# A post-LayerNorm layer whose SBUF buffers start at other offsets: products' operands at multiples of 2,048 bytes

## The reference

```python
q = (x @ Wq.T + bq).reshape(B, S, H, D)      # k, v alike; H = 16, D = 32; q, k get rotary
qk = jnp.einsum('bshd,bstd->bsht', q, k) / jnp.sqrt(jnp.float32(D))
att = jax.nn.softmax(qk, axis=-1)
out = jnp.einsum('bsht,bstd->bshd', att, v)
out = jnp.swapaxes(out, 1, 2).reshape(B, S, E)
x = _layernorm(x + out @ Wo.T + bo)
g = jnp.einsum('th,ih->ti', xf, gate_w) * gate_s
u = jnp.einsum('th,ih->ti', xf, up_w) * up_s
hdn = jax.nn.silu(g) * u
x = _layernorm(x + jnp.einsum('ti,hi->th', hdn, down_w) * down_s)
```

## Time and profile before

| | |
|---|---|
| three runs | 1808.6, 1810.26 and 2465.16 us, median 1810.26 |
| profiled execution | 1810.45 us, of it the span from first to last instruction 1808.7 us |
| TensorE clock over the span | 0.981 of full |
| busy: TensorE, VectorE, ScalarE, GpSimd | 96%, 76%, 52%, 45% of the span |
| DMA | 278 MB, 154 GB/s over the span |

### The profile page before, as it was taken

The page is one execution under the profiler, slowest core; times in us unless marked ns, Lnnn a source line. Parts: engine busy times, 40 slices in busy tenths (PEclk is TensorE's granted clock), DMA queues, the critical chain, the costliest instruction groups (busy, mean ns, idle before and its releaser), DMA issues.

```text
span 1808.7 us, 40710 instructions
## 1 busy us (share of the span) xinstructions
PE 1731.1 (96%) x15138; PEld 1412.3 (78%) x15138; DVE 1375.9 (76%) x1976; ACT 943.2 (52%) x1458; POOL 809.2 (45%) x697
## 2 busy tenths in 40 slices
PE   4799999999999999999789999999999999999997
PEld 3677888888888888888568888888888888788785
DVE  5587999999999999999745766667666676667656
ACT  4354555555556555655534555455555545555453
POOL 5587888888888888888100110201102011020111
PEclk8799999999999999999989999999999999999998
DMA  5747668767786778678564353553436435254241
GB/s 162 150 96 168 163 154 177 175 162 155 172 175 167 158 165 176 169 161 209 165 208 148 117 178 96 184 167 126 153 96 203 148 130 164 82 200 148 92 164 70
DMA packets 447479, 278.20 MB, mean 154 GB/s; under 512 B 261440, under 2 KB 385984, under 8 KB 447424
## 3 DMA queue, kind: packets, MB, share of 16 engines
q1 hardware_dynamic: 447424, 277.50, 57.3%
HBM read 184.10 MB, written 93.32 MB: 153 GB/s over the span
## 4 chain that ended last, share of the span: by engine, by line
PE 91%; issue 3%; SPq 1%; DVE 1%; ACT 1%; DMA 1%; POOL 1%; POOLq 0%; ACTq 0%; DVEq 0%
PE ps_x L582 13%; PE ps_x L586 12%; PE ps_x L583 12%; PE ps_s L715 8%; PE ps_s L720 8%; PE ps_x L715 7%; PE ps_x L720 7%; PE ps_x L726 4%; PE ps_x L730 4%; PE ps_s L659 3%; PE ps_a L616 3%; PE ps_s L726 2%; PE ps_a L730 2%; PE ps_a L726 2%; PE ps_s L730 2%
## 5 line engine op out<-in xcount | busy, mean ns | idle before, releaser
L582 PE MATMUL ps_x<-wqkv_hi,xc_hi 128*128 128x512 f32 x768 | 307.1, 400 | 19.6 <-POOL xc_lo L1061 8.0
L586 PE MATMUL ps_x<-wqkv_hi,xc_lo 128*128 128x512 f32 x768 | 302.6, 394 | 0.0
L583 PE MATMUL ps_x<-wqkv_lo,xc_hi 128*128 128x512 f32 x768 | 302.5, 394 | 0.0
L1171 POOL TENSOR_TENSOR z<-z,xr 128x512 f32<-128x512 f32 x60 | 77.4, 1319 | 496.6 <-DVE z L1436 496.6
L715 PE MATMUL ps_s<-x_hi,slot 128*128 128x512 f32 x672 | 268.1, 399 | 7.9 <-ACT hid L949 4.5
L720 PE MATMUL ps_s<-x_lo,slot 128*128 128x512 f32 x672 | 265.5, 395 | 0.0
L861 ACT ACTIVATE kX<-kT 32x512 f32<-32x512 f32 x256 | 160.7, 628 | 188.2 <-DVE kT L1242 185.9
L1082 POOL TENSOR_TENSOR qk_cos<-qk_in,rot 128x512 f32<-128x512 f32 x128 | 202.4, 1581 | 83.2 <-DVE qk_in L1221 65.4
L715 PE MATMUL ps_x<-x_hi,slot 128*128 128x512 f32 x560 | 222.5, 397 | 6.7 <-ACT u L978 3.7
L720 PE MATMUL ps_x<-x_lo,slot 128*128 128x512 f32 x560 | 220.8, 394 | 0.0
L1088 POOL TENSOR_TENSOR qk_cos<-qk_cos,qk_sin 128x512 f32<-128x512 f32 x128 | 205.4, 1605 | 10.0
(11 more groups left out here) (112 smaller groups left out, 3724.6 us busy)
## 6 DMA issues: line engine op xcount, KB each, us to landing
slot<-gu_hi SPq DMA_DIRECT2D x88, 896.0 KB, 5.1
xc<-x_cols SPq DMA_DIRECT2D x32, 512.0 KB, 5.4
v_rows<-v_in SPq DMA_DIRECT2D x32, 512.0 KB, 4.2
v<-v_rows SPq DMA_DIRECT2D x32, 512.0 KB, 5.2
res<-x_rows SPq DMA_DIRECT2D x64, 256.0 KB, 3.5
x_rows<-x_out SPq DMA_DIRECT2D x32, 512.0 KB, 2.8
x_cols<-x_turn SPq DMA_DIRECT2D x128, 128.0 KB, 2.6
wide<-x_cols SPq DMA_DIRECT2D x64, 256.0 KB, 5.1
```

The lines of the kernel that those rows point to most:

```text
L582: pe.matmul(out, hi[:, k], w_hi[w][:, k], start=(k == 0), stop=False)
L583: pe.matmul(out, hi[:, k], w_lo[w][:, k], start=False, stop=False)
L586: last = pe.matmul(out, lo[:, k], w_hi[w][:, k], start=False, stop=(k == KE - 1))
L1171: pool.tensor_tensor(z[:, h, r], z[:, h, r], xr[:, r], ALU.add).then_inc(z_added[h], 1)
```

## The change

Only the order in which buffers are declared changes. The instructions of every engine, their order and their waits are the same as before, row by row; what differs is the addresses in them.

```diff
         inexact = sb("inexact", [P, 1], mybir.dt.int32)
-        wide = sb("wide", [P, 2, 4, E])
-        slot0 = sb("slot0", [P, OPS, HALF], F32R)
         gu_scale = sb("gu_scale", [P, 2, NJ])
...
         own4 = sb("own4", [P, A4])
-        rot = sb("rot", [P, 2, 2, D])
         stats = sb("stats", [P, 2, 6])
...
         ones = sb("ones", [P, 1])
+        to_line = sb("to_line", [P, 112])
+        wide = sb("wide", [P, 2, 4, E])
         w_raw = raw = wide
...
             prob = sb("prob", [P, 2 * Q32, H], F32, early)
-            top, total, over = (sb(name, [P, 2 * Q32], F32, early) for name in ("top", "total", "over"))
             pT = sb("pT", [P, 2, C * B4, Q32], F32, early)
...
         h1 = sb("h1", [P, 2, E], F32R)
-        rest1 = sb("rest1", [P, 3, 2 * Q32])
         h2, h3 = sb("h2", [P, 2, E], F32R), sb("h3", [P, 2, E], F32R)
         xr = sb("xr", [P, ROWS, E])
+        slot0 = sb("slot0", [P, OPS, HALF], F32R)
+        rot = sb("rot", [P, 2, 2, D])
+        top, total, over = (sb(name, [P, 2 * Q32]) for name in ("top", "total", "over"))
```

## The result

The changed kernel takes 1800.73 us (median of 5 runs, 1798.35 to 1802.78) where the kernel before takes 1809.81: a ratio of 0.9953, 95% interval 0.994 to 0.9965, that is 9.1 us or 0.5% less. One of the five executions of the kernel before took 2465.16 us and is not in the ratio. The forecast was 1,802.5. Its size and its place were right. Its reason, a border within 64 bytes, was not, as the experiments show.

The account below looks back on a forecast made before the run. The prediction took the distance between TensorE matmuls to bound the kernel. From 1,810.45 us it subtracted 7.9 us for slot0 and nothing for other operands, engines or DMA, giving 1,802.5 us, range 1,797 to 1,811.

Parts of the forecast that it names:

- a border within 64 bytes: Large matmuls: operands starting off a multiple of 64 are slow; only slot0 did, costing 9 ns a matmul.
- What bounds the kernel: Whole kernel: the distance between TensorE matmuls sets the time, while VectorE keeps its spare 8% in attention.
- Part 1: Feed-forward stage: slot0's matmuls reach the other slots' distance once at a multiple of 2,048; 7.9 us gained, bounds 5.5 to 8.4.
- 3 x 0.26 + 0.2: Gain per super step, in us: 0.26 for each of chunks 3, 6 and 9, and 0.2 for chunk 0.
- Part 2: Other large matmul operands, both stages: moving to multiples of 512 or 2,048 gains nothing; bound 92 us.
- the number of matmuls in a window: Attention's 200 us window: over 2,554 matmuls there would show that the other operands' starts gained time after all.
- Part 3: VectorE, ScalarE and GpSimd operands: new addresses change nothing; VectorE's 1,220 and GpSimd's 1,581 ns stay.
- Part 4: DMA targets: offsets change within 256 bytes; loads landing tenths of a microsecond earlier are covered by TensorE's work, gain nothing.
- A: Large matmuls: the start of moving or all operands costs 13.3 ns each; expected 1,710 to 1,740 us, chance 13%.
- B: slot0 in the feed-forward stage: low place or chunk turn, not address, makes it slow; 1,810 us, chance 9%.
- The rule of 16-byte cachelines: SBUF starts: a multiple of 32 is as good as 2,048, so moving slot0 gives nothing; 1,810 us.
- C: Attention, GpSimd and VectorE: operands with one remainder clash and slow the kernel to 1,830 to 1,850 us; chance 3%.

Follow-up runs that it names:

- e1: Kernel before with only slot0 declared 32 bytes later, at 192 of 2,048: 1808.12 us, ratio 0.9995 to the kernel before.
- e3: Changed kernel with everything from wide on 32 bytes later, so all large matmul operands start 32 past a multiple of 64: 1801.2 us, 0.9957 of before.
- e2: Changed kernel with slot0 alone 32 bytes later, 32 past a multiple of 2,048: 1807.92 us, ratio 0.9992 to the kernel before.
- e5: Kernel before with only slot0 declared behind z_shift, at 576 of 2,048: 1801.2 us, ratio 0.9961 to the kernel before.
- e6: Changed kernel with slot0's seven weight tiles at a pitch of 1,056 instead of 1,024 bytes: 1803.91 us in one run.
- e8: Kernel before with the chunks of moving operand wd at a pitch of 2,080 instead of 2,048 bytes: 1813.19 us in one run, against 1808.06 before.

## Why the prediction was right, and where it was not

**What bounds the kernel.** Right. TensorE's distance between starts sets the time, and every effect that was found acts through it. VectorE (183.81 of 200 us in the same window of attention, 183.32 before) and the others have not moved.

**Part 1, slot0.** The size was right: a super step lost 1.00 us where the sum had 3 x 0.26 + 0.2 = 0.98. It is earned in seven super steps, not eight: from the first to the second it was 139.1 us before and is 139.3; attention's rest is mixed in there. In the thirteen traces that stretch takes 137.1 to 139.8 us, so a gain of 1 us in it would not be seen. So the term is 7.0 us as far as it is shown, where 7.9 were taken; the prediction's lower bound had allowed for this. The reason was wrong. The step that failed is "what sets `slot0` apart is its address", 32 past a multiple of 64. The rows could not tell that from another reading, since `slot0` was at the same time the only stationary operand whose distance from its moving one was no multiple of 256 (96, against 0 and 256). The prediction looked at addresses one by one and never subtracted them. e1, at a multiple of 64 and slow, and e3, off it and fast, show it. That the size came out all the same is luck in one respect: the change also brought `slot0` and `x_hi` to one remainder, for which the prediction had no reason. e1 fulfils its rule without that and was 0.7 us under the kernel before, within the noise.

**Part 2, all other operands.** Nothing was taken and nothing came: attention's twelve matmuls from 508.58 to 511.30 us in the changed kernel take the same 2.72 us.

```profile
508.58 0.39 PE L582 MATMUL ps_x<-wqkv_hi,xc_hi 128*128 128x512 f32 x1
508.81 0.39 PE L583 MATMUL ps_x<-wqkv_lo,xc_hi 128*128 128x512 f32 x1
...
511.30 0.39 PE L582 MATMUL ps_x<-wqkv_hi,xc_hi 128*128 128x512 f32 x1
```

The argument for it, that these operands respect a border of 64 already, falls with part 1; the right one is that all of them lay at one remainder of 256 before too, 64. The sign that the prediction named beside it, the number of matmuls in a window, was a poor one: the window of 300 to 500 us holds 2,675 matmuls instead of 2,554, only because 128 more of the small ones of line 616 fall into it; of the large ones it holds 754 instead of 760.

**Part 3, the other engines.** Right, nothing:

```profile
L1422 DVE TENSOR_TENSOR x_lo<-wide,x_hi 128x1024 fp32r<-128x1024 f32 x32 | 38.9, 1220 | 1.3 <-ACT x_hi L997 1.3
L1082 POOL TENSOR_TENSOR qk_cos<-qk_in,rot 128x512 f32<-128x512 f32 x128 | 202.5, 1582 | 81.9 <-DVE qk_in L1221 63.9 <-DVE kT L1242 18.0
```

**Part 4, DMA.** Not contradicted for the time, and blind to what happens. The loads of `slot0` and the other slots, of `xc` and of `v` land 0.3 to 0.8 us earlier in the median (below), under cover of TensorE's work.

**The other 2 us.** The profiled executions differ by 9.8 us, of which super steps give 7.0. The feed-forward stage began at 874.1 us before and at 871.2 after. In the other profiled kernels of this study it began anywhere from 869.0 to 874.0, and in three executions of the full change at 871.2, 873.2 and 869.0. e1, with the late landings of the old layout, began at 872.6, not later than the repeated full change beside it with 873.2. This part is scatter of a single execution as far as the runs show.

**The rivals.** A fell: the matmuls stayed at 226.7 ns, in e3 and at multiples of 2,048 alike; what the 13.3 ns over 213.3 are is still open. B, that the address is not the cause, fell in its form of place and turn (e2 has the new place and is slow, e5 the old region and is fast), yet it came nearest to the truth in that the address by itself isn't the cause. The rule of 16-byte cachelines from the Trainium skill, "SBUF — State Buffer", section "Door 1: The DMA port swizzle", was set beside it: a start at a multiple of 32 is indeed as good as one at 2,048, as e3 shows, but two such starts 32, 96 or 128 bytes apart cost 7 to 9 ns a matmul, of which that rule tells nothing. C did not occur.

## What to carry to other kernels

Keep the stationary and the moving operand of a stream of matmuls at one remainder of 256 bytes; at the remainders 0, 32 and 64 that were run it made no difference where both lie, and 2,048 is not needed. One small tensor declared ahead of a weight buffer can cost 3 to 4% of each matmul that reads the buffer, with no wait that tells it, rows that read 0.40 instead of 0.39 us, and a busy time of 199.9 of 200 us either way; the distance between starts, compared between buffers, shows it. When an outlier has a special address, subtract it from the addresses that it is used with before believing in the address itself, and test by moving all together, then one alone.

## What the runs showed of the hardware beside that

That a distance costs anything was not foreseen: 7 to 9 ns of 226.7 in fp32r matmuls of 128 by 512 columns, gone at 256 bytes. Why, no run shows; reads of the two operands that get into each other's way would do that, but this is only argued. One thing in the traces bears on it: with `slot0` 128 bytes off (e1) or 32 off (e2), the distance *ahead* of its first matmul in chunk 3 is already long, 232.6 and 235.0 ns (means over seven super steps; 226.7 in the changed kernel). In single rows of e1, 0.24 us lie ahead of the first `slot0` matmul at 1253.41:

```profile
1252.95 0.39 PE L715 MATMUL ps_x<-x_hi,slot 128*128 128x512 f32 x1
1253.17 0.40 PE L720 MATMUL ps_x<-x_lo,slot 128*128 128x512 f32 x1
1253.41 0.40 PE L715 MATMUL ps_s<-x_hi,slot 128*128 128x512 f32 x1
```

So the pair that matters may be the moving operand of one matmul and the stationary one of the *next*. But at 64 bytes (e6) the distance ahead is 225.9 ns, and in e8, where the moving operand was moved, 226.9; no run separates the two readings. How far all this holds for other types or sizes was not tried.

The DMA engines answer to the layout too. Their part of the page, changed kernel:

```profile
q1 hardware_dynamic: 447424, 277.50, 54.1%
xc<-x_cols SPq DMA_DIRECT2D x32, 512.0 KB, 4.7
v<-v_rows SPq DMA_DIRECT2D x32, 512.0 KB, 4.4
```

and e3, the same layout 32 bytes later:

```profile
q1 hardware_dynamic: 447424, 277.50, 57.5%
xc<-x_cols SPq DMA_DIRECT2D x32, 512.0 KB, 5.3
v<-v_rows SPq DMA_DIRECT2D x32, 512.0 KB, 5.2
```

The columns are packets, MB and the engines' busy share, then for each load its count, size and median us to landing. Before it was 57.3%, 5.4 and 5.2. With the same bytes in the same packets the engines are busy for 3 points less, and these two loads land 0.6 to 0.8 us earlier, when most buffers start at multiples of 2,048. All thirteen traces agree: 54.0 to 54.4% in the seven with the new layout, 57.3 to 57.8% in the five with the old one and in e3. Most of the difference lies in short packets: those of 128 bytes took 16.0 ns on average and take 13.0, those of 2,048 bytes 93.8 and 92.2. Whether a multiple of 2,048 is needed or a smaller one would do, no run shows. The Trainium skill, "DMA: Bandwidth & Descriptors", section "How a descriptor splits into AXI transactions", says that a transaction must start at a multiple of 256 bytes, so that a descriptor that starts elsewhere fetches bytes that it doesn't use; the direction agrees, with most buffers 64 past such a multiple before, 32 in e3 and 0 in the changed kernel. No gain in time from it is shown here, where the loads lie under TensorE's work. A kernel that waits for DMA might gain from it, which no run here shows.
